# A recommendation tower on one core: fewer GpSimd pairs in the first two blocks, gathers spread anew, and GpSimd's pairs taken third and fifth

## What is computed

```python
x0 = xk = e                                    # (1024, 32, 16)
for W in (W0, W1, W2):                         # (32, h, 64), h = 32, 64, 64
    xk = relu(einsum('bmd,bhd,mhk->bkd', x0, xk, W))
    outs.append(sum(xk, axis=2))
z = concatenate(outs, axis=1)                  # (1024, 192)
h = relu(concatenate([z, dense_ctx], 1) @ W_top1 + b_top1)
h = relu(h @ W_top2 + b_top2)
y = h @ W_top3
```

## Time and profile before

| what | value |
|---|---|
| median of 3 runs | 665.54 us (663.15 to 666.22) |
| the profiled execution, its time | 662.89 us |
| its span, first to last instruction | 661.1 us |
| TensorE (PE) busy | 605.5 us, 92% |
| VectorE (DVE) busy | 569.6 us, 86% |
| GpSimd (POOL) busy | 453.1 us, 69% |
| ScalarE (ACT) busy | 358.0 us, 54% |
| mean granted clock of TensorE | 0.974 of full speed |

### The profile page before, as it was taken

How to read it: one execution, slowest core, us unless ns; L and a number is a source line. 1 busy time by engine, 2 the same in 40 slices (tenths; PEclk the granted TensorE clock), 3 DMA queues, 4 the chain that set the end, 5 groups by cost and what they waited for, 6 DMA issues and landing times. The chain is left out here.

```text
span 661.1 us, 9151 instructions
## 1 busy us (share of the span) xinstructions
PE 605.5 (92%) x3172; PEld 247.5 (37%) x3172; DVE 569.6 (86%) x336; ACT 358.0 (54%) x669; POOL 453.1 (69%) x307
## 2 busy tenths in 40 slices
PE   4499849979999999989999999999999999999988
PEld 3352313224343344424343344434443443434434
DVE  5759975986989899897989899898989898999863
ACT  0184922817647392927647392928556482829251
POOL 6786887888869694888869697787877070716220
PEclk9689969989999999999999999999999999999989
DMA  6899679797695969698694969688795869492000
GB/s 186 190 240 278 150 213 214 217 216 193 146 248 142 208 199 214 193 200 237 141 255 137 213 193 211 193 198 225 180 258 131 186 217 217 155 214 41 1 0 1
DMA packets 60175, 119.82 MB, mean 181 GB/s; under 512 B 15271, under 2 KB 33734, under 8 KB 60054
## 3 DMA queue, kind: packets, MB, share of 16 engines
q1 hardware_dynamic: 41798, 111.02, 67.1%
q10 hardware_dynamic: 10768, 6.53, 3.7%
q0 software_dynamic: 7584, 1.96, 3.0%
HBM read 115.27 MB, written 5.25 MB: 182 GB/s over the span
## 5 line engine op out<-in xcount | busy, mean ns | idle before, releaser
L483 DVE TENSOR_TENSOR z_dve<-xq,x0b 128x2048 f32<-128x2048 f32 x209 | 464.5, 2283 | 68.4 <-ACT xq L637 39.2
L879 PE MATMUL acc<-z_dve,w_cin 128*64 128x512 f32 x1672 | 379.2, 597 | 11.1 <-DVE z_dve L483 10.8
L439 POOL TENSOR_TENSOR z_pool<-x0b,xs 128x2048 f32<-128x2048 f32 x47 | 213.5, 4558 | 108.2 <-ACT xs L637 107.2
L423 POOL DMA_INDIRECT emb<-in_tbl_dram,ids_all x224 | 220.0, 982 | 72.0 <-issue 70.3
L879 PEld LDWEIGHTS acc<-z_dve,w_cin 128*64 128x64 f32 x1672 | 122.4, 137 | 234.9 <-issue 186.5
L645 ACT ACTIVATE xq<-acc 32x512 f32<-32x512 f32 x256 | 144.6, 565 | 3.4
L637 ACT ACTIVATE xq<-acc 64x512 f32<-64x512 f32 x128 | 73.0, 570 | 119.8 <-DVE z_dve L483 62.8
L879 PE MATMUL acc<-z_pool,w_cin 128*64 128x512 f32 x376 | 90.6, 615 | 16.1 <-POOL z_pool L439 16.1
L637 ACT ACTIVATE xs<-acc 64x512 f32<-64x512 f32 x128 | 75.7, 591 | 1.9
L483 DVE TENSOR_TENSOR z_dve<-xq,x_rot 128x2048 f32<-128x2048 f32 x30 | 67.2, 2281 | 0.0
L879 PE MATMUL acc<-z_dve,w_sym 128*64 128x512 f32 x256 | 58.0, 593 | 0.2 <-DVE z_dve L483 0.2
(11 more groups left out here) (97 smaller groups left out, 229.2 us busy)
## 6 DMA issues: line engine op xcount, KB each, us to landing
x0b<-x0t SPq DMA_DIRECT2D x120, 512.0 KB, 14.5
x_rot<-x0t SPq DMA_DIRECT2D x60, 512.0 KB, 6.2
x_rep<-x0t SPq DMA_DIRECT2D x15, 512.0 KB
x0b<-x0t SPq DMA_DIRECT2D x16, 256.0 KB, 7.2
emb<-in_tbl_dram,ids_all POOLq DMA_INDIRECT x224
x0t<-emb_t ACTq DMA_DIRECT2D x28, 128.0 KB
w_cin<-in_L_rec_W_dram SPq DMA_DIRECT2D x16, 64.0 KB
x_lo<-x0t SPq DMA_DIRECT2D x15, 64.0 KB
```

The lines of the kernel that those rows point to most:

```text
L423: nc.gpsimd.indirect_dma_start(out=rows[:, D * f:D * f + D], out_offset=None, in_=tables[f], in_offset=bass.IndirectOffsetOnAxis(ap=ids_al ...
L439: nc.gpsimd.tensor_tensor(z_pool[:, n % ZP_SLOTS, :, :], x0b[b % 2][:, 2 * j:2 * j + 2, :], xs[l - 1][:, :].unsqueeze(1).broadcast_to([P, ...
L483: nc.vector.tensor_tensor(z_dve[:, base % Z_SLOTS, :, :], in0.unsqueeze(1).broadcast_to([P, 2, N]), in1, ALU.mult).then_inc(z_made, 1)
L879: ins = nc.tensor.matmul(acc[l][K * side:K * side + K, :], weights[c], z[:, c, NH * side:NH * side + NH], start=start and c == 0, stop=sto ...
```

## The change

GpSimd makes no pair of layer 1 in block 0 and only NAT 0 in block 1, so VectorE makes one more in each. The gathers of these blocks are spread anew; both versions have issued 62 by the end of block 1. TensorE's order of layer 1 has GpSimd's pairs third and fifth (in block 1 the one left is third), where they were first and second. Half 1 of tile 1 is turned after the third pair of layer 2 in block 0, and ScalarE's `move_half(1, 1)` stands ahead of `set_relu(1)` and `x1_swp`. `x1_pool` of block 0 falls away, and the counts of `xs_x1_ready` are one lower.

```diff
     def pool_l1(b):
-        return (3,) if b == 0 else (0, 1)
+        return () if b == 0 else (0,) if b == 1 else (0, 1)
...
     def gathers(b):
-        return (9, 1, 12) if b == 0 else (0, 14, 8) if b == 1 else (0, 14, 2)
+        return (14, 2, 8) if b == 0 else (3, 11, 6) if b == 1 else (0, 14, 2)
...
         if b == 0:
-            return [(NAT, 0), (NAT, 1), (NAT, 2), (SWP, 0), (SWP, 1), (SWP, 2), (NAT, 3), (SWP, 3)]
-        return [(NAT, 0), (NAT, 1), (SWP, 0), (SWP, 1), (SWP, 2), (SWP, 3), (NAT, 2), (NAT, 3)]
+            return [(NAT, 0), (NAT, 1), (NAT, 2), (NAT, 3), (SWP, 0), (SWP, 1), (SWP, 2), (SWP, 3)]
+        if b == 1:
+            return [(SWP, 0), (SWP, 1), (NAT, 0), (SWP, 2), (SWP, 3), (NAT, 1), (NAT, 2), (NAT, 3)]
+        return [(SWP, 0), (SWP, 1), (NAT, 0), (SWP, 2), (NAT, 1), (SWP, 3), (NAT, 2), (NAT, 3)]
...
                 n1, n2, n3 = gathers(b)
-                pool.wait_ge(xs_x1_ready, b + 1)
+                if b > 0:
+                    pool.wait_ge(xs_x1_ready, b)
...
                     x2_swp(t, k)
                     if not last:
                         x1_pool(t, k + 1)
+                    if k == 0 and first_tile:
+                        move_half(1, 1)
...
                         x1_swp(t, k + 1)
...
-                    if k == 0 and first_tile:
-                        move_half(1, 1)
...
             x1_nat(0, 0)
             x1_swp(0, 0)
-            x1_pool(0, 0)
...
                         cin_pair(2, t, k, v, j, i)
-                        if i == 6 and k == 0 and first_tile:
+                        if i == 2 and k == 0 and first_tile:
                             pe.wait_ge(emb_copied, 1)
                             transpose_half(1, 1)
```

More of the change, by code:

```diff
@@ L500, in add_relu @@
                 if l == 0:
-                    dve.wait_ge(xs_x1_ready, 2 * t + 2)
+                    dve.wait_ge(xs_x1_ready, 2 * t + 1)
                     dve.wait_ge(x1_ready[NAT], 2 * t + 2)
@@ L663, in x1_pool @@
                 act.wait_ge(*acc_done(0, t, k))
-                if blk(t, k) > 0:
+                if blk(t, k) > 1:
                     act.wait_ge(*pool_made(1, t, k - 1))
@@ L863, in claim @@
                 if l == 0:
-                    pe.wait_ge(xs_x1_ready, 2 * t + k)
+                    if blk(t, k) > 1:
+                        pe.wait_ge(xs_x1_ready, 2 * t + k - 1)
                     pe.wait_ge(x1_ready[NAT], 2 * t + k)
```

## The result

The changed kernel took 655.38 us (median of 4, 653.34 to 659.0) against 664.38 for the kernel before on the same chip: ratio 0.9865, 95% interval 0.9834 to 0.9896. Measured once more, beside some of its parts (after_third), it was 653.95 against 664.93: 0.9841 (0.9801 to 0.9881). So it is faster by 9 to 11 us, on the predicted side and inside the range, but 5 to 6 us short of the 649.2 that I forecast. Each comparison left a profile; their spans are 657.2 (the first) and 651.9 us (after_third), against 661.1 before. A third, from a slower chip, follows with the experiments.

A forecast was written before the change was run, and what follows sets the result against it. TensorE sets the pace; its early waits for GpSimd's pairs cost at most 18.2 us. Gains of 8.6 + 5.9 + 1.8 = 16.3 us from the 665.54 median give 649.2 us, range 645 to 656 for 8 in 10.

The forecast's parts named there:

- Block 1: Layer 1 of block 1: VectorE makes seven products, GpSimd one; the layer ends at 102.95, not 111.57, 8.6 us earlier.
- Block 2, layer 1: TensorE's new order, with VectorE no longer stalled, starts NAT 3 at 137.3, not 151.79: 14.5 us won by there.
- term of 5.9 us: The part of the 14.5 us won by NAT 3 of block 2 that is won in block 2 itself.
- rival 1: Only block 1 pays: loads or gathers come late in block 2, the 5.9 us stay lost; 656.9 us, chance 0.10.
- term of 1.8 us: Block 6: with GpSimd's NAT 1 in fifth place, TensorE's 1.81 us wait after GpSimd's 8.04 us gap between gathers goes.
- Rival 2: The gain is given back later: DMA queues become the bound and the middle stretches; near 665.5 us, chance 0.03.
- Rival 3: TensorE's clock falls to 1.2 GHz while following VectorE, costing 11 us in block 1; 660.2 us, chance 0.03.
- Rival 4: VectorE's SWP 0 is late at layer 1 heads in blocks 3 to 15; 675.2 us at 2 us each, chance 0.03.
- rival 5: More than forecast, below 645 us: the remaining 0.3 to 0.7 us rests per tile close as well; chance 0.03.
- The moved transposition: Block 0, layer 2: x1_swp ends at 84.5, just covered by VectorE's work; tile 1 is in memory some 6.5 us earlier.
- the 1.0 us to spare: Head of layer 1, block 4: VectorE's SWP 0 ends at about 211.6, TensorE comes at 212.63, so no cost.

The follow-up runs named there:

- e2: Changed kernel with block 3's x0b load held until VectorE has made layer 0 of block 3; ratio 0.9878 to the kernel before, on a slower chip.
- e5: Changed kernel with tile 1's half 1 transposition and `move_half(1, 1)` back at their old places; 662.30 us, ratio 0.9964 to the kernel before, faster chip.
- e1: Changed kernel with two more gathers in block 1 ahead of the extra piece (5, 11, 6); ratio 0.9861 to the kernel before, on a slower chip.

## Why the prediction was right, and where it fell short

| step, us earlier than before | predicted | first profile | after_third |
|---|---|---|---|
| end of layer 1, block 1 (111.57 before) | 8.6 | 8.45 | 7.95 |
| start of NAT 3, block 2 (151.79 before) | 14.5 | 8.2 | 11.4 |
| start of layer 0 of block 3 (153.56 before) | 14.5 | 6.5 | 11.4 |
| the tile with the gap (75.36 before) | 1.8 | -2.0 | -1.7 |
| span (661.1 before) | 16.3 | 3.9 | 9.2 |

Block 1 came out as worked: VectorE's eighth product, the waits of a few tenths, x1_swp just ahead of VectorE's need, GpSimd's pair. Only x_hi was late for GpSimd in the first profile. after_third started layer 1 of block 0 0.45 us later, hence 7.95.

The number held partly by luck: the first median lies 0.6 us inside the upper end of my range, and two of its four runs outside it (656.1 and 659.0).

The step that failed is the one in "Block 2, layer 1" that runs "NAT 2, the transposition, NAT 3 at 137.3". TensorE was at the transposition in time, but I let its rows be there. For tile 1 I had taken 4.3 us for a gather's landing, from tile 0's gathers; for tile 2 I never asked, though its last two gathers leave at 132.84 and 134.13, under a full DMA load. In the kernel before these two left at 141.48 and 142.77, and the five pairs behind NAT 1 stood between them and the transposition at 151.42; with NAT 1 in fifth place only two do. The price was 5.26 us of rest and 1.7 us of low clock in the first profile, 2.47 us in after_third. So the term of 5.9 us was worth nothing in one execution (8.2 - 8.45) and 3.4 in the other (11.4 - 7.95). The row that should have warned me is the share of 1.05 in the earlier trace rows: rival 1 names loads or gathers for it, but I worked it out for x0b alone. e2 shows that the load is what makes them late. No variant of the changed kernel on the faster chip was without this wait, so its price rests on the two profiles above.

The term of 1.8 us had the wrong sign for the same reason. The gap came back and NAT 1 was not waited for, as argued, but GpSimd's delay hit the next thing it owes: the last two gathers of that half tile. The tile lost 1.7 to 2.0 us more than before.

Rival 1, only block 1 pays, gave 656.9 and comes nearest to the measured 655.4. It named loads or gathers that come late in block 2, and gathers it was; that its 5.9 us were then lost held in the first profile. Its path was another: VectorE's layer 1 of block 2 was not late, and no load of x0b or x_rot was, but TensorE's transposition waited. Rival 2, given back later, holds for 2 us of it. Rival 3 did not occur: the clock stayed at 1.00 while TensorE followed VectorE, with rests of at most 0.7 us between pairs. The Trainium skill's rule on frequent brief idling (TensorE: Matmul & The Clock Gate, "A second HAM failure mode: psum-queue depth-cycling") is not borne out by this trace. Rival 4 did not occur either: no wait for `z_dve` over 1 us at a head of layer 1. Nor did rival 5.

The moved transposition I had priced at nothing but 0.2 us and an earlier load. e5 shows that 8 us hang on it, by the chain tile 1 in memory, x_hi, extra piece, gathers, GpSimd's multiplies. My chain had all these links, but I did not run it backwards to see what they cost without the move.

Two readings were off without harm. In the earlier trace rows the 8 of the middle stands in slice 19, and the last two slices have 8 too. In block 4, VectorE's row of four holds two products of layer 2 and two of layer 1, so SWP 0 is its third and not its last; the time of 211.6 and the 1.0 us to spare are right for the third.

Open: whether two gathers sooner wins back the missing 5 to 6 us where the kernel takes 655 us; why its gain is lost again behind the wait on the slower chips; what makes these slower; what the 8 us gap is.

## What to carry to other kernels

When a wait is taken away, list what the waiting engine asks for next, and when each of these was issued, not only when it was used: a transfer that always came in time may have come in time only behind the old wait. An engine that is short of time over several stages was not helped here by a new order of its work, only by less of it, or by feeding it sooner. A small gather that shared the DMA engines with a 4 MB load landed late; issued before the load (e1), it was there in time, though on the slower chips the kernel gained nothing by it.

## What the runs showed of the hardware

- A gather of 32 packets landed within 5.1 us of its issue with the DMA engines at a share of 0.08 (e2). Where TensorE waited for one beside a load (12 waits in 8 profiles, shares of 0.79 to 1.04), it had its rows 7.7 to 10.2 us after the issue; in the first profile, at a share of 1.03, none of its packets moved for 6 us.
- A rest of 2.47 us did not lower TensorE's clock (next pair 1.94 us), one of 1.99 us later in the same execution did (next pair 3.41 us), and so did rests of 3.94 us in the kernel before (next pair 3.58 us), 5.26 and 8.74 us. The same kernel ran with mean clocks of 0.977 to 0.987 on the chip of the first result.
- GpSimd stood 8.0 to 8.2 us between two gathers, ahead of the same gather in all kernels with 62 gathers issued by the end of block 1, on faster and slower chips, and not in the one with 64.
- On two chips every kernel took about 13% longer than on the faster one (the kernel before 754.91 and 757.17 us against 664.93).
